# Weights folded at the last tile of statistics, a bias table from one selection matrix, and a reordered set-up of attention, in a two-layer block on one core

## The chip, the core and the metric

The kernel runs on one NeuronCore of a Trainium2 chip. The core has five engines with instruction streams of their own: TensorE (PE) multiplies matrices into PSUM, VectorE (DVE), ScalarE (ACT) and GpSimd (POOL) work elementwise, and SyncE (SP) issues most transfers; ACT can issue transfers too. Sixteen DMA engines carry the transfers. Engines wait for each other on semaphores only. The metric is the device time of one execution in microseconds (us). The kernel before takes 4699.47 us, the median of three runs (4699.33 to 4706.42).

## What is computed

The input x is 16 images of 56 x 56 pixels and 192 channels in float32. Two layers follow, each behind a group norm (32 groups over an image) and each added to its input:

```
x = x + L0(_gn(x))
x = x + L1(_gn(x))

L0(x): windows of 7 x 7 pixels; w = _ln(w, ln1_w, ln1_b)
       h_t = (w_t @ Bm) + h_(t-1) @ A          # over the 49 pixels of a window
       w = h @ Cm;  y = _ln(w, ln2_w, ln2_b)
       return w + gelu(y @ W1 + b1) @ W2 + b2
L1(x): roll by (-3, -3), windows of 7 x 7
       q, k, v = split(xw @ qkv_w.T + qkv_b)   # 12 heads of 16
       attn = q @ k.T / 4 + rpb_table[rel_idx] + shift_mask
       out = softmax(attn) @ v @ proj_w.T + proj_b;  roll back
```

`rpb_table` has 169 rows (13 x 13 relative positions) of 12 heads. `rel_idx` picks a row for each pair of the 49 pixels of a window, so the bias table of a head is 49 x 49.

## The kernel before

The program has three blocks, one after the other. At the end of a block every engine waits for all the others.

**Statistics of layer 0 and its weights.** x is read as 8 tiles of 128 windows by 49 pixels by 192 channels, 4.82 MB each. SP issues a load per tile into a ring of three buffers `xs` (line 147); the load of tile k waits until DVE has finished tile k - 2 (`s_bn`). DVE runs 32 BN_STATS on a tile, one per group (L204). The eleven loads of weights are issued by ACT on its own queue (L155, L157). Ahead of tile NT // 2, which is tile 4, DVE waits for all of them (`s_w`) and scales Bm and W1 by the weights of the layer norms (L198, L199). ACT then writes the upper parts of the weights (L162, L163) and POOL the lower parts (L175, L177); PE computes biases (L247, L251). After the last tile DVE, PE and POOL turn the statistics into tables (L208 to L235; POOL's power is L180).

**Layer 0.** 98 steps of 512 tokens. The last thing that a step does is the sum `x1` on DVE (L491). SP then stores it with 14 transfers (L379), seven for each half q of the partitions, into `x1_cells` in DRAM, while POOL adds it and its square to `acc_x` and `acc_x2` (L463 to L468). SP waits for the landing of all stores before the block ends (L383).

**Layer 1.** Its set-up stands in the code engine by engine. SP loads `hot0`, `hot1` (a one-hot matrix of 169 x 49 x 49, split at 128 rows), `groups`, `tab0`, `tab1` (the 169 rows of the table) and `mask`, all on semaphore `s_l` (L811), then the weights on `s_w3` (L816). It waits for `s_par`, and loads the tokens of units 0 and 1 and their parameters (L825, L826). DVE reduces the accumulators (L1024), PE averages over windows (L1130), DVE and POOL make mean and rstd (L1030 to L1036, L868), PE waits for all six of `s_l` and spreads them to channels (L1137), DVE copies (L1042, L1043), and PE projects the shifts through the weights (L1149) once `s_w3` is full. DVE makes `params` (L1050, L1052) and signals `s_par`. PE then gathers the bias table: for each of the 49 keys m two matmuls, `hot0` against `tab0` and `hot1` against `tab1`, with 12 columns (L1155, L1156). DVE meanwhile zeroes buffers (L1054 to L1059), copies the gathered table to both halves of the partitions (L1065) and adds the four masks (L1070), which sets `s_tabs`. PE waits for `s_tabs` before its first transposes (L1177). From there 256 units of four window pairs follow, of which nothing is changed.

## Time and profile before

| | us or share |
|---|---|
| median of three runs | 4699.47 |
| the profiled execution's own time | 4700.3 |
| its span | 4698.5 |
| statistics and weights, up to the first work of layer 0 | 0 to 151 |
| layer 0 | 151 to 2440.9 |
| set-up of layer 1 | 2440.9 to 2502 |
| units of layer 1 | 2502 to 4698.5 |
| busy shares: PE, DVE, ACT, POOL | 95%, 78%, 53%, 55% |
| mean granted clock of TensorE | 0.988 |

The busy shares are means over blocks that differ. PE's 95% is made in the 98 steps and the 256 units. In the slices of the page PE shows a 0 at the start and a 6 in the middle, which are the two places where it has next to nothing to do: the statistics and the set-up of layer 1. Times below are us from the start of the span. The execution takes 1.8 us more than its span.

### The profile page before, as it was taken

What the parts mean: (1) busy time and instruction counts of PE and PEld (TensorE: products, weight loads), DVE (VectorE), ACT (ScalarE), POOL (GpSimd) and SP (SyncE); (2) the same over time, 40 slices, a digit from 0 to 9 for tenths busy, and PEclk for the clock granted to TensorE, in tenths of its full rate; (3) what the DMA queues carried; (4) which work ended last, traced back from release to release, by engine and by line L of the source; (5) the groups of instructions that cost most, each with busy time, mean ns of one, the idle gap of its engine ahead of it and who ended that gap; (6) DMA issues with size and microseconds to landing.
All of it is one profiled execution on the core that took longest, in us unless ns stands there. A gap on an engine that the chain in (4) does not pass through costs nothing. (4 is left out here: it accounts for less than half of the span.)

```text
span 4698.5 us, 139967 instructions
## 1 busy us (share of the span) xinstructions
PE 4477.9 (95%) x51720; PEld 3760.2 (80%) x51720; DVE 3655.4 (78%) x7082; ACT 2497.3 (53%) x4850; POOL 2583.0 (55%) x2098
## 2 busy tenths in 40 slices
PE   0599999999999999999969999999999999999999
PEld 0488888888888888888857888888888888888887
DVE  6798888888888888888845777777777777777776
ACT  0244444444444444444424666666666666666666
POOL 1154455455445545545544666666666666666666
PEclk9999999999999999999988999999999999999999
DMA  8011111111111111111111222222222222222222
GB/s 346 22 39 38 38 38 40 39 39 41 38 38 39 39 39 39 41 38 38 40 45 48 73 72 70 72 72 70 71 71 70 71 72 72 72 70 72 72 70 62
DMA packets 389801, 286.01 MB, mean 61 GB/s; under 512 B 147163, under 2 KB 388043, under 8 KB 388555
## 3 DMA queue, kind: packets, MB, share of 16 engines
q1 hardware_dynamic: 387012, 283.15, 20.8%
q10 hardware_dynamic: 2736, 2.14, 0.1%
q8 instruction: 35, 0.57, 0.1%
q14 instruction: 18, 0.15, 0.0%
HBM read 120.34 MB, written 87.31 MB: 44 GB/s over the span
## 5 line engine op out<-in xcount | busy, mean ns | idle before, releaser
L894 POOL TENSOR_TENSOR L<-L,mx 128x588 f32<-128x588 f32 x512 | 601.3, 1175 | 747.7 <-DVE mx L1108 741.4
L1104 DVE SCALAR_TENSOR_TENSOR L<-ps_s,bias 128x588 f32<-128x588 f32 x512 | 394.7, 771 | 457.7 <-PE ps_s L1168 453.8
L603 PE MATMUL ps_o<-w,g_hi 128*128 128x384 f32 x2352 | 710.2, 365 | 5.9 <-DVE g_lo L543 4.1
L415 ACT ACTIVATE gF<-ps_g,b1f 128x512 f32<-128x512 f32 x588 | 405.9, 690 | 393.0 <-PE ps_g L634 390.5
L888 POOL TENSOR_TENSOR E<-E,ri 128x588 f32<-128x588 f32 x512 | 600.5, 1173 | 3.1 <-DVE ri L1114 3.1
L603 PE MATMUL ps_o<-w,g_lo 128*128 128x192 f32 x2352 | 534.4, 254 | 0.0
L975 ACT ACTIVATE PT<-ps_t 98x588 f32<-98x588 f32 x512 | 343.3, 671 | 325.9 <-PE ps_t L1243 322.9
L442 POOL TENSOR_TENSOR res<-xt,b2b 128x768 f32<-128x768 f32 x98 | 181.1, 1848 | 591.2 <-DVE x L491 591.2
L1168 PE MATMUL ps_s<-Kp,Q 32*64 32x98 f32 x12288 | 494.0, 259 | 3.6 <-DMA Kp<-K 2.7
L401 ACT ACTIVATE h_hi<-ps_h,hbias 128x512 fp32r<-128x512 f32 x196 | 123.3, 680 | 702.8 <-PE ps_h L618 702.8
L603 PEld LDWEIGHTS ps_o<-w,g_hi 128*128 128x128 f32 x2352 | 429.3, 189 | 26.5 <-issue 24.5
L603 PEld LDWEIGHTS ps_o<-w,g_lo 128*128 128x128 f32 x2352 | 443.8, 191 | 0.0
L1168 PEld LDWEIGHTS ps_s<-Kp,Q 32*64 32x64 f32 x12288 | 297.5, 130 | 158.2 <-issue 100.1
L1108 DVE TENSOR_REDUCE mx<-L 128x12 f32<-128x588 f32 x512 | 392.3, 766 | 17.5
L998 ACT ACTIVATE oT<-ps_v,vb 128x98 f32<-128x98 f32 (+1 forms) x1024 | 290.3, 335 | 216.4 <-PE ps_v L1275 216.4
L1217 PE MATMUL ps_w<-wp,oT 128*98 128x192 f32 x2048 | 396.3, 337 | 0.9 <-ACT oT L998 0.9
L1112 DVE TENSOR_REDUCE sm<-E 128x12 f32<-128x588 f32 x512 | 386.7, 755 | 1.5 <-ACT E L981 1.5
L1275 PEld LDWEIGHTS ps_v<-PT,Vx 98*32 98x32 f32 x12288 | 310.6, 150 | 93.6 <-issue 49.1
L1275 PE MATMUL ps_v<-PT,Vx 98*32 98x49 f32 x12288 | 374.7, 235 | 2.4 <-ACT PT L975 2.2
L452 POOL TENSOR_TENSOR g_lo<-gF,g_hi 128x512 fp32r<-128x512 f32 x196 | 251.1, 1303 | 198.6 <-ACT g_hi L420 198.6
L420 ACT ACTIVATE g_hi<-gF 128x512 fp32r<-128x512 f32 x588 | 355.4, 621 | 0.0
L981 ACT ACTIVATE E<-L 128x588 f32<-128x588 f32 x512 | 351.2, 686 | 3.6 <-POOL L L894 0.4
(210 smaller groups left out, 11761.5 us busy)
## 6 DMA issues: line engine op xcount, KB each, us to landing
xs<-in_x SPq DMA_DIRECT2D x8, 4704.0 KB, 22.5
xt<-in_x SPq DMA_DIRECT2D x98, 384.0 KB, 3.4
x_cells<-x SPq DMA_DIRECT2D x784, 48.0 KB
xb<-x_cells SPq DMA_DIRECT2D x128, 294.0 KB
Vx<-V SPq DMA_DIRECT2D x512, 73.5 KB
out<-yo SPq DMA_DIRECT2D x128, 294.0 KB
Kp<-K SPq DMA_DIRECT2D x256, 98.0 KB, 2.0
Kp<-K SPq DMA_DIRECT2D x256, 49.0 KB, 1.9
```

Of the source, the lines that this page charges most:

```text
L415: act.activation(gF[f % 4][:, :], ps_g[:, f % 2, :], ACT.Gelu, bias=b1f[:, f:f + 1]).then_inc(s_gelu, 1)
L420: act.activation(g_hi[:, g, :], gF[g % 4][:, :], ACT.Copy).then_inc(s_gh, 1)
L603: last = pe.matmul(dst, g[:, f, P * k:P * (k + 1)], w, start=(f == 0 and i == 0), stop=(f == FT - 1 and i == 1))
L888: pool.tensor_tensor(e, e, ri[p][:, :].unsqueeze(2).to_broadcast([P, HEADS, T]), ALU.mult)\
L894: pool.tensor_tensor(l, l, mx[p][:, :].unsqueeze(2).to_broadcast([P, HEADS, T]), ALU.subtract).then_inc(s_sub, 1)
L981: act.activation(E[pp][:, :, :], L[pp][:, :, :], ACT.Exp).then_inc(s_ex, 1)
L1104: dve.scalar_tensor_tensor(out=L[p][:, :, :].rearrange("p (a h) m -> p a (h m)", a=2), in0=ps_s[:, :, 0:SB], scalar=HD ** -0.5, in1=tab, o ...
L1108: dve.tensor_reduce(mx[p][:, :], L[p][:, :, :], AX.X, ALU.max).then_inc(s_mx, 1)
L1112: dve.tensor_reduce(sm[pp][:, :], E[pp][:, :, :], AX.X, ALU.add).then_inc(s_sm, 1)
L1168: last = pe.matmul(s_pair(j)[SLOT * w:SLOT * (w + 1)], Q[c][rows, chunk, 2 * p + w, :], Kp[c][rows, chunk, :, 2 * p + w, :], start=True, s ...
L1217: last = pe.matmul(ps_w(OUT1 if half else OUT0)[0:T2, C * a:C * (a + 1)], oT[d][p][:, k, :], wp[:, k, :], start=(k == 0), stop=(k == 1))
L1275: last = pe.matmul(ps_v[row:row + 2 * HD, col:col + T], Vx[lc][0:T2, 2 * lp + w, g:2 * HD * JP:JP], PT[lp % 2][0:T2, j, T * w:T * (w + 1)] ...
```

## The change

There are four edits.

1. DVE's wait for the weights and the folding stand ahead of the last tile of statistics (tile 7), no longer ahead of tile 4.
2. The seven stores of half q = 1 of the very last step are issued by ACT, which first waits for `s_x1`; SP issues the seven of q = 0. The code of a store becomes a function, which is otherwise the same.
3. The bias table is selected in another way. The table is loaded reversed. `tab` has 85 partitions by 49 keys by 12 heads: partition p holds for each key the row of the table that lies p rows behind the key's own first row. Four transfers write it. A matrix `query_row` of 85 x 128 has one 1 per query (for both halves of the partitions). Two matmuls of 504 and 84 columns then give the whole table, and two copies instead of four take it out. `hot0`, `hot1`, `tab0` and `tab1` are gone.
4. The set-up is in another order. PE gathers first, ahead of the averaging, and so waits for all seven loads of `s_l` before anything else. DVE zeroes its buffers in its waits, and its `base` copies stand ahead of the table of shifts. SP issues the tokens of unit 0 before its wait for `s_par`.

```diff
-                        if k == NT // 2:
+                        if k == NT - 1:
 
                             dve.wait_ge(s_w, 16 * WEIGHT_LOADS)
...
-                        for q in range(2):
+                        for q in range(1 if isinstance(n, int) and n == STEPS else 2):
+                            store(sp, d, u, q)
...
                 slots(act, slot)
+                act.wait_ge(s_x1, STEPS)
+                store(act, (STEPS - 1) % CHUNKS, (STEPS - 1) // CHUNKS, 1)
...
-            hot0, hot1 = sb("hot0", [P, T, T]), sb("hot1", [RPB - P, T, T])
-            tab0, tab1 = sb("tab0", [P, HEADS]), sb("tab1", [RPB - P, HEADS])
+            SPAN = 2 * WS - 1
+            REACH = (WS - 1) * (SPAN + 1) + 1
+            query_row, tab = sb("query_row", [REACH, P]), sb("tab", [REACH, T, HEADS])
...
+                for high in ((SHIFT, WS), (0, SHIFT)):
+                    for wide in ((SHIFT, WS), (0, SHIFT)):
+                        ny, nx = high[1] - high[0], wide[1] - wide[0]
+                        first = SPAN * ((high[0] - SHIFT) % WS) + (wide[0] - SHIFT) % WS
+                        rows = bass.AP(rpb.tensor, rpb.offset + HEADS * first,
+                                       [[HEADS, REACH], [HEADS * SPAN, ny], [1, nx * HEADS]])
+                        sp.dma_start(tab[:, :, :].rearrange("p (i j) h -> p i (j h)", i=WS)
+                                     [:, high[0]:high[1], HEADS * wide[0]:HEADS * wide[1]], rows).then_inc(s_l, 16)
...
-                sp.wait_ge(s_par, 1)
...
                     sp.dma_start(xb[c][0:T2, :, :], src).then_inc(s_xb[c], 16)
+                    if isinstance(u, int) and u == 0:
+                        sp.wait_ge(s_par, 1)
...
+                dve.memset(Kp[1][:, :, :, :, :], 0.0)
+                dve.memset(Vx[0][:, :, :], 0.0)
+                dve.wait_ge(s_b2, 1)
+                for b in range(2):
+                    m0, m1 = MB * b, min(MB * (b + 1), T)
+                    last = dve.tensor_copy(base[:, :, m0:m1],
+                                           ps_b[:, b, 0:(m1 - m0) * HEADS].rearrange("p (m h) -> p h m", h=HEADS))
+                link(last)
                 dve.wait_ge(s_p2, 1)
...
+                pe.wait_ge(s_l, 16 * 7)
+                for b in range(2):
+                    m0, m1 = MB * b, min(MB * (b + 1), T)
+                    last = pe.matmul(ps_b[:, b, 0:(m1 - m0) * HEADS], query_row[:, :],
+                                     tab[:, m0:m1, :].rearrange("r m h -> r (m h)"), start=True, stop=True)
+                last.then_inc(s_b2, 1)
                 pe.wait_ge(s_v2, 1)
...
-                for m in range(T):
-                    dst = ps_b[0:T, m // MB, (m % MB) * HEADS:(m % MB + 1) * HEADS]
-                    pe.matmul(dst, hot0[:, m, :], tab0[:, :], start=True, stop=False)
-                    last = pe.matmul(dst, hot1[:, m, :], tab1[:, :], start=False, stop=True)
-                last.then_inc(s_b2, 1)
```

DVE in the first block, before. `xs` are the tiles of x, `fold_B` and `fold_1` the scaled weights:

```order
L204 BN_STATS st<-xs2 128x6 x32
L204 BN_STATS st<-xs0 128x6 x32
L198 TENSOR_SCALAR fold_B<-raw_B,l1 128x192
L199 TENSOR_SCALAR fold_1<-raw_1,l2 128x768
L198 TENSOR_SCALAR fold_B<-raw_B,l1 128x192
L199 TENSOR_SCALAR fold_1<-raw_1,l2 128x768
L204 BN_STATS st<-xs1 128x6 x32
L204 BN_STATS st<-xs2 128x6 x32
L204 BN_STATS st<-xs0 128x6 x32
L204 BN_STATS st<-xs1 128x6 x32
L208 TENSOR_TENSOR pm<-st 128x256
```

The same stretch of DVE now:

```order
L204 BN_STATS st<-xs2 128x6 x32
L204 BN_STATS st<-xs0 128x6 x32
L204 BN_STATS st<-xs1 128x6 x32
L204 BN_STATS st<-xs2 128x6 x32
L204 BN_STATS st<-xs0 128x6 x32
L198 TENSOR_SCALAR fold_B<-raw_B,l1 128x192
L199 TENSOR_SCALAR fold_1<-raw_1,l2 128x768
L198 TENSOR_SCALAR fold_B<-raw_B,l1 128x192
L199 TENSOR_SCALAR fold_1<-raw_1,l2 128x768
L204 BN_STATS st<-xs1 128x6 x32
L208 TENSOR_TENSOR pm<-st 128x256
```

The four instructions that need the weights moved behind three more tiles of statistics.

PE in the set-up of layer 1, before, from its first instruction. `ps_w` and `ps_s` are PSUM; of L1155 and L1156 there are 49 pairs:

```order
L1130 MATMUL ps_w<-img_mean,pm 32x2 x16
L1137 MATMUL ps_w<-tab,groups 128x32
L1137 MATMUL ps_w<-tab,groups 64x32
L1149 MATMUL ps_w<-shift,raw_qkv 128x16 x6
L1149 MATMUL ps_w<-shift,raw_qkv 32x16 x12
L1155 MATMUL ps_s<-tab,hot 49x12
L1156 MATMUL ps_s<-tab,hot 49x12
```

PE there now:

```order
L1139 MATMUL ps_s<-tab,query_row 128x504
L1139 MATMUL ps_s<-tab,query_row 128x84
L1145 MATMUL ps_w<-img_mean,pm 32x2 x16
L1151 MATMUL ps_w<-tab,groups 128x32
L1151 MATMUL ps_w<-tab,groups 64x32
L1163 MATMUL ps_w<-shift,raw_qkv 128x16 x6
L1163 MATMUL ps_w<-shift,raw_qkv 32x16 x12
L1186 MATMUL ps_w<-ident,xb 128x98 x4
```

Two gathering matmuls stand first, and the transposes of unit 0 follow right behind the projection of the shifts.

SP's loads on `s_l`, before and then now:

```order
L811 DMA hot<-in_onehot 128x2401
L811 DMA hot<-in_onehot 41x2401
L811 DMA groups<-in_group_of 32x192
L811 DMA tab<-in_rpb 128x12
L811 DMA tab<-in_rpb 41x12
L811 DMA mask<-in_shift_mask 128x196
```

```order
L820 DMA tab<-in_rpb 85x4x48
L820 DMA tab<-in_rpb 85x4x36
L820 DMA tab<-in_rpb 85x3x48
L820 DMA tab<-in_rpb 85x3x36
L823 DMA query_row<-in_query_of 85x128
L823 DMA groups<-in_group_of 32x192
L823 DMA mask<-in_shift_mask 128x196
```

The one-hot rows are gone; four transfers of short runs (48 or 36 values) stand in their place.

## Rows read from the trace of the kernel before

**Rows 1.** Timeline of the first block: start, us, engine, line, operation [idle before <-releaser]

```profile
14.72 46.90 DVE L204 BATCH_NORM_STATS2 st<-xs 128x6 f32<-128x294 f32 x128 [14.72 <-DMA xs<-in_x]
...
88.51 0.32 DVE L198 TENSOR_SCALAR fold_B<-raw_B,l 128x192 f32<-128x192 f32 x1 [26.89 <-DMA raw<-in_W]
...
90.16 46.90 DVE L204 BATCH_NORM_STATS2 st<-xs 128x6 f32<-128x294 f32 x128
...
101.27 2.61 POOL L177 TENSOR_TENSOR w<-raw,w 128x1152 fp32r<-128x1152 f32 x1
...
143.42 1.02 POOL L180 TENSOR_TENSOR gtab<-gvar,neg_half 128x4 f32<-128x4 f32 x1 [39.53 <-DVE gvar L227]
```

**Rows 2.** DMA queues from 10 to 60 us: packets, MB, share of 16 engines

```profile
q1 hardware_dynamic: 638, 21.04, 97.8%
q10 hardware_dynamic: 639, 0.36, 2.3%
```

**Rows 3.** Stretches: length, five engines' busy time, PEclk, DMA share, GB/s

```profile
70.00:80.00 10.00, 0.00 (x0) 0.00 (x0) 0.00 (x0) 0.00 (x0) 0.00 (x0) 1.00 1.00 431
80.00:85.00 5.00, 0.00 (x0) 0.00 (x0) 0.00 (x0) 1.28 (x1) 0.00 (x0) 1.00 0.79 269
```

**Rows 4.** Timeline at the end of layer 0, SP's queue and POOL

```profile
2430.43 8.88 SPq L379 DMA_DIRECT2D x_cells<-x  x14
...
2433.62 1.80 POOL L468 TENSOR_TENSOR acc_x<-acc_x,x1sq 128x768 f32<-128x768 f32 x1
...
2440.92 0.72 SPq L811 DMA_DIRECT2D hot<-in_onehot  x2
```

**Rows 5.** Timeline of the set-up of layer 1

```profile
2442.96 10.54 SPq L811 DMA_DIRECT2D mask<-in_shift_mask  x1
...
2444.43 1.87 PE L1130 MATMUL ps_w<-img_mean,pm 128*32 128x2 f32 x32 [15.25 <-DVE pm L1024]
...
2447.24 2.90 POOL L868 TENSOR_TENSOR tab<-var,neg_half 32x16 f32<-32x16 f32 x1 [11.81 <-DVE var L1034]
...
2462.97 0.97 PE L1137 MATMUL ps_w<-tab,groups 32*128 32x32 f32 x4 [16.68 <-DMA mask<-in_shift_mask]
...
2464.95 5.99 PE L1149 MATMUL ps_w<-shift,raw_qkv 128*128 128x16 f32 x36 [1.01 <-DMA pbb<-in_proj_b]
...
2470.87 0.34 PE L1155 MATMUL ps_s<-tab,hot 128*49 128x12 f32 x2
...
2471.41 0.25 DVE L1052 COPY params<-ps_w 128x16 f32<-128x16 f32 x2
...
2472.08 0.55 SPq L826 DMA_DIRECT2D par<-params  x1
...
2473.74 1.36 DVE L1056 MEMSET Kp<- 128x1568 f32 x1 [0.28 <-issue]
...
2475.76 1.34 DVE L1059 MEMSET Vx<- 128x1536 f32 x1 [0.37 <-issue]
...
2497.24 1.67 DVE L1065 COPY base<-ps_s 49x504 f32<-49x504 f32 x4 [18.53 <-PE ps_s L1156]
...
2498.94 2.81 DVE L1070 TENSOR_TENSOR bias<-base,mask 128x588 f32<-128x588 f32 x4
...
2501.97 1.54 PE L1177 MATMUL ps_w<-ident,xb 98*128 98x98 f32 x8 [4.76 <-issue]
```

**Rows 6.** Stretches while the loads on `s_l` run; columns as in rows 3

```profile
2444.00:2445.00 1.00, 0.57 (x11) 0.58 (x12) 0.37 (x1) 0.00 (x0) 0.00 (x0) 0.50 1.06 451
...
2447.00:2449.00 2.00, 0.00 (x0) 0.00 (x0) 0.16 (x1) 0.00 (x0) 1.76 (x1) 0.50 0.07 29
```

**Rows 7.** SP's DMA queue, 2622.7 to 2623.2 (packets of 384 B) and 2438 to 2439 (mostly 768 B)

```profile
q1 hardware_dynamic: 116, 0.04, 35.3%
...
q1 hardware_dynamic: 112, 0.07, 29.5%
```

**Rows 8.** The costliest groups, page part 5: line, engine, operation, count | busy, mean ns

```profile
L1217 PE MATMUL ps_w<-wp,oT 128*98 128x192 f32 x2048 | 396.3, 337 | 0.9 <-ACT oT L998 0.9
```

More of the change, by code:

```diff
@@ L340, in there, with store @@
                 return not isinstance(n, int) or 0 <= n < STEPS
+            def store(engine, d, u, q):
+                i = u // WS
+                a, b = (WS + SHIFT - 1 - i) // WS, (WS + SHIFT - 1 - u % WS) // WS
+                imgs = slice(2 * TPC * d + q, 2 * TPC * (d + 1), 2)
+                base = q * WINS
+                rows, cols = bass.ds(1 - a, CELLS), bass.ds(1 - b, CELLS)
+                row, col = bass.ds(CELLS + 1 - a, 1), bass.ds(CELLS + 1 - b, 1)
+                parts = [(x1[d][base:base + WINS, k, :],
+                          x1_cells[rows, imgs.start + 2 * k, cols, bass.ds(u, 1), :]
+                          .rearrange("r w t c -> r w (t c)")) for k in range(TPC)]
+                parts += [(x1[d][base:base + CELLS, :, :],
+                           x1_cells[row, imgs, cols, bass.ds(u, 1), :]
+                           .rearrange("r k w t c -> (r w) k (t c)")),
+                          (x1[d][base:base + WINS:CELLS, :, :],
+                           x1_cells[rows, imgs, col, bass.ds(u, 1), :]
+                           .rearrange("r k w t c -> (r w) k (t c)")),
+                          (x1[d][base:base + 1, :, :],
+                           x1_cells[row, imgs, col, bass.ds(u, 1), :]
+                           .rearrange("r k w t c -> (r w) k (t c)"))]
+                for src, dst in parts:
+                    engine.dma_start(dst, src).then_inc(s_st[d], 16)
             block = ctx.enter_context(nc.Block())
@@ L808, in _ @@
             def _(sp):
-                for dst, src in ((hot0[:, :, :], onehot[0:P]), (hot1[:, :, :], onehot[P:RPB]),
-                                 (groups[:, :], group_of), (tab0[:, :], rpb[0:P]), (tab1[:, :], rpb[P:RPB]), (mask[:, :, :], shift_mask)):
+                for high in ((SHIFT, WS), (0, SHIFT)):
[6 more added lines that the diff above has]
+                                     [:, high[0]:high[1], HEADS * wide[0]:HEADS * wide[1]], rows).then_inc(s_l, 16)
+                for dst, src in ((query_row[:, :], query_of), (groups[:, :], group_of), (mask[:, :, :], shift_mask)):
                     sp.dma_start(dst, src).then_inc(s_l, 16)
@@ L1026, in _ @@
                 link(last)
+                dve.memset(Q[1][:, :, :, :], 0.0)
+                dve.memset(wp[CB:P, 1, :], 0.0)
+                link(dve.memset(params[:, :, :], 0.0))
                 dve.wait_ge(s_m2, 1)
```

56 lines of the change are left out of this document (11 added, 45 removed).

## Prediction

> **What bounds the kernel now.** I read the slices of the page first. PE is at nine tenths or more nearly everywhere, and none of its work there is edited, so the steps and units of both layers should keep their 4.49 ms. What can move is what lies between: the first 151 us and the middle. I read these in the timeline, then the DMA queues beside them.
>
> In the first block DVE sets the pace. It has 46.90 us of BN_STATS for four tiles, 11.73 us a tile, then sits idle for 26.89 us until the weights land at 88.51, folds for 1.65 us, and takes another 46.90 us [rows 1]. The weights are late because they share the engines with x: from 10 to 60 us x moved 638 packets and the weights 639 [rows 2], one for one, at 37.6 KB against well under 1 KB. The wait is thus for the stream of x to dry up, and it dries up because DVE waits: the DMA share is 1.00 up to 80 us and 0.79 in the next five [rows 3].
>
> At the end of layer 0 SP issues 14 stores in 8.88 us, one each 0.63 us; the next block begins 1.61 us behind the last of them, at 2440.92 [rows 4]. POOL was done at 2435.42.
>
> The set-up of layer 1 takes 61.05 us from there to the first transposes at 2501.97 [rows 5]. Its chain is: the loads on `s_l`, which PE awaits until 2462.97; a further DMA wait; the projection of 5.99 us; 98 gathering matmuls from 2470.87 to 2497.2; the copies of 1.67 us; the masks of 2.81 us [rows 5]. The load that holds everything is the one-hot part with 41 partitions: at first all 16 engines are busy (share 1.06), then for some ten us the share is 0.07 at 29 GB/s, one engine of 16 [rows 6].
>
> **Edit 1, the folding.** DVE reaches tile 7 at 14.72 + 7 x 11.73 = 96.8. Is x there in time? Tile 7 may be requested when tile 4 is done, at 73.4, while the stream is still full. It is 4.82 MB, at 431 GB/s [rows 3] 11.2 us, and lands some 11 us behind the end of the stream near 81, about 92 to 93: in time. The weights now wait behind that tile as well: 88.51 + 11.2, less about 0.3 for the eight weight packets per engine that slip through beside it, is 99.4. So DVE idles from 96.8 to 99.4, folds until 101.1, and ends tile 7 at 112.8, where it ended at 137.06 before. **Gain 24.3 us.** ACT's and POOL's splitting now lies behind the fold: POOL ended 103.88, 13.7 us behind the fold's end at 90.16 [rows 1], so it would end at 114.8. The power on POOL is due 6.3 us behind the last tile (137.1 to 143.42) [rows 1], at 119.1; the cover is 4.3 us, and if it went, every us beyond would cost one. PE's biases take 8 us and are hidden likewise. Bounds: 22, if the weights land at 101.7, and 26.9, if DVE's idle time vanishes altogether.
>
> **Edit 2, the stores.** SP's seven take 4.43 us, until 2434.9. ACT's seven run beside them; no row shows ACT issuing such a store, so between SP's 0.63 us each and, if the two queues hindered each other fully, the old 8.88 us for both. A packet of 768 B keeps an engine busy 0.295 x 16 x 1 us / 112 = 42 ns [rows 7]; 648 packets over the 8 rows that a store spans are 3.4 us, less than the issue time, so I take 0.63 to 0.7. The block then starts near 2435.2 + 1.6 = 2436.8; POOL's end at 2435.42 is the floor. **Gain 4.1 us**, bounds 0 and 4.9. Behind ACT's new wait nothing is queued, since these were its last instructions of the block.
>
> **Edit 3, the new loads.** This is the dear unknown. The four transfers of `tab` have 85 x 14 = 1190 runs of 192 or 144 B. Two things are needed: the cost of a packet and the number of engines. Packets of 384 B take 0.353 x 16 x 0.5 us / 116 = 24 ns of an engine [rows 7], and shorter ones should not be dearer by much. From above, engine 0 had still 59 small packets behind the one-hot rows (41 x 9.6 KB at 29 GB/s, to about 2459.4) and all had landed by 2462.97, so no more than 61 ns each [rows 5, 6]. I take 30, nearer to the measured packet. On the engines: 128 partitions used all sixteen, 41 used one [rows 6]. I read that as a cut into equal shares of partitions; 85 is 5 x 17, so five engines with 238 packets each, 7.1 us. With 1.5 us until data flows, 27 packets more for `query_row`, `groups` and `mask` (0.9 us) and about 0.5 to 1 us of landing, `s_l` is full **10.0 us** after the block's start (call it L). At 24 ns it is 8.9, at 61 ns 18.6.
>
> The Trainium skill, "DMA: Bandwidth & Descriptors", section on why a DMA increments its semaphore by 16, says that the engine count is the largest number up to 16 that divides the slowest dimension of both sides. By that rule, the trace agrees: 41 gives one. Without any such rule, spread evenly over sixteen, L would be 5.4 and the sum 4.6 us better. Under "Specifications" the same page says that a transfer under 512 B costs a read-modify-write. The row of 384 B does not show it, at 24 ns against 42 for 768 B; were each short packet doubled to 48 ns, L would be 14.8 and the sum 4.8 us worse.
>
> **Edit 4, the new chain**, from the block's start, with handovers of about 0.1 us. All terms but three are from [rows 5]:
> - L, 10.0. PE now waits for it before everything. DVE's reduction (3.41 us) and three memsets are over by 5.4, so the averaging, which ran at 3.5 before, is what is queued behind that wait. This costs the chain 6.5 us plus the gather.
> - The gather: 588 columns. An f32 matmul of 192 columns takes 337 ns at the full clock [rows 8], and the clock here is 0.50 [rows 6], thus 3.5 ns a column: 2.1.
> - Averaging 1.87, then DVE's four small steps until POOL could start, 0.94.
> - POOL's power 2.90 is now beside DVE's two memsets, 1.36 + 1.34, and two copies, half of 1.67, with gaps 4.1. The longer, 4.1, counts. One small step, 0.23.
> - L1137's matmuls 1.07; DVE's copies and the handover, at most the 1.01 that stood there.
> - The projection 5.99 + 0.1. Its weights on `s_w3` are issued once the queue drains, near L - 2, and need some 6 to 7 us, by 15; the projection is due at 21. Hidden, with 6 us of cover.
> - `params` 0.72; the masks 2.81 + 0.07; handover 0.22. The load of `par` (0.55 and at most the 1.6 us that a store takes to land [rows 4]) is beside the masks, and the tokens of unit 0 are already there.
>
> The sum is 31.1 us, against 61.05: **gain 29.9 us**. What leaves is the gather of 26.3 us and most of a 16.68 us wait; what comes is the wait for `tab`. With L from 8.9 to 18.6 the gain is 31.0 to 21.3. PE's clock is at 0.50 in this stretch before, and I expect it there again, with no change for unit 0.
>
> **Sum.** 24.3 + 4.1 + 29.9 = 58.3 us. The profiled execution took 4700.3, so 4642.0; it lies 0.8 us above the median of the runs, so **4641 us**.
>
> **Rivals.**
> - **`tab` comes late.** If the 1190 packets went over one engine as those of 41 partitions did, they take 28.6 us at 24 ns and L is about 32: 22 us worse, 4663. Five engines at 100 ns a packet give nearly the same. For it: no row shows such short runs from DRAM spread over a count like 85. Against: 48 B rows were taken at under 61 ns.
> - **The weights stay starved.** ACT's queue refills only as it drains, and DVE waits for weights to 110 instead of 99.4. Then 4652. For it: the last weights were requested only at 81, when x dried up. Against: from there to the landing took 7.5 us, and nothing slows that now.
> - **The long loops shift.** Their buffers have other addresses and another start. They are 95% of the time; 0.2% of them is 9 us, either way: 4632 or 4650. Against: no instruction in them differs.
> - **Slower.** A packet of `tab` costs a full round of its engine, with nothing overlapped. The only packets seen alone on an engine, the 9.6 KB ones, took 326 ns. At that price 265 packets take 86 us, L is 89 and the kernel 4720. It decides from 68 us for L, about 250 ns a packet. Against: the 384 B rows at 24 ns.
> - **Nothing is won at the start.** DVE's idle time moves whole behind tile 6. That needs weights at 123, with nothing on the queues by then: left at 0.01 or less.
>
> **How the numbers follow.** Forecast 0.76, `tab` late 0.11, weights starved 0.05, loops 0.04 (half each way), slower 0.03, nothing at the start 0.01. The forecast's own bounds add to 22 + 0 + 21.3 and 26.9 + 4.9 + 31.0, but not all ends meet at once; 4634 to 4656 holds them. The range reaches from 4632 to 4659, which leaves out most of the late `tab` and the slower case. A difference under 0.2%, 9.4 us, could not be told from no change. Faster by more: 0.96; within: 0.01; slower: 0.03.
>
> **What would show it.** DVE idle for some 3 us ahead of L198, near 97, and the first step of layer 0 near 127. The set-up's first transfer near 2412 on the new clock (24 + 4 us earlier than 2440.92). The two gathering matmuls about 10 us behind it, released by DMA. The first transposes 31 us behind it, released by DVE's masks. I would be wrong if the DMA view showed `tab` at one engine's share for 20 us and more, if POOL's L180 waited for L177, or if the 256 units took another time than 2196.5 us.

## The result: 4643.9 us, and the profile after

The changed kernel takes 4643.86 us, median of four runs (4638.18 to 4645.91), against 4702.94 for the kernel before on the same chip (4699.33 to 4706.47). The ratio is 0.9872, 95% interval 0.9855 to 0.989: faster by 59 us. The forecast was 4641 us, range 4632 to 4659. The profiled execution of the changed kernel took 4643.41 us, with a span of 4641.6.

The span of before is 4698.5. The 56.9 us between the two spans lie here:

| stretch | before | after | gain | forecast |
|---|---|---|---|---|
| start to the first load of layer 0 | 151.33 | 129.93 | 21.4 | 24.3 |
| from there to the end of the last x1 | 2279.03 | 2279.76 | -0.7 | 0 |
| x1 to the first transfer of the next block | 10.56 | 7.16 | 3.4 | 4.1 |
| block's start to the first transposes | 61.05 | 26.23 | 34.8 | 29.9 |
| the 256 units and the end | 2196.5 | 2198.5 | -2.0 | 0 |

First the timeline of the first block in the changed kernel (start, us, engine, line, operation; in brackets the idle time before it and what ended it). It answers to [rows 1].

```profile
100.47 0.32 DVE L198 TENSOR_SCALAR fold_B<-raw_B,l 128x192 f32<-128x192 f32 x1 [3.54 <-DMA raw<-in_W]
...
113.23 2.61 POOL L177 TENSOR_TENSOR w<-raw,w 128x1152 fp32r<-128x1152 f32 x1
113.94 2.36 DVE L208 TENSOR_TENSOR pm<-st 128x256 f32<-128x256 f32 x1
116.33 0.61 DVE L209 TENSOR_TENSOR sq<-st 128x256 f32<-128x256 f32 x1
...
122.02 1.02 POOL L180 TENSOR_TENSOR gtab<-gvar,neg_half 128x4 f32<-128x4 f32 x1 [6.18 <-DVE gvar L227]
```

DVE's wait of 26.89 us has become one of 3.54. The line to look at is DVE's L208, though: L208 and L209 have the same shape and the same kind, and one took 2.36 us, the other 0.61. L208 was due while POOL had its subtract of 2.61 us in hand, and ended 0.46 us after it.

Now SP's and ACT's queues at the end of layer 0 and the start of the next block; this answers to [rows 4].

```profile
2409.72 5.51 ACTq L363 DMA_DIRECT2D x_cells<-x  x7
2409.76 4.54 SPq L363 DMA_DIRECT2D x_cells<-x  x7
...
2416.85 2.19 SPq L820 DMA_DIRECT2D tab<-in_rpb  x4
...
2420.06 0.41 SPq L823 DMA_DIRECT2D mask<-in_shift_mask  x1
```

A store costs ACT 5.51 / 7 = 0.79 us to issue, where SP needs 0.65, and the block begins 1.6 us behind ACT's last. The mask's issue, which took 10.54 us before [rows 5], takes 0.41: the queue no longer blocks.

The set-up of layer 1, in order of time; this answers to [rows 5].

```profile
2422.16 2.40 PE L1139 MATMUL ps_s<-tab,query_row 85*128 85x504 f32 x4 [13.65 <-DMA mask<-in_shift_mask]
2424.49 1.87 PE L1145 MATMUL ps_w<-img_mean,pm 128*32 128x2 f32 x32
...
2427.30 2.90 POOL L880 TENSOR_TENSOR tab<-var,neg_half 32x16 f32<-32x16 f32 x1 [12.55 <-DVE var L1049]
...
2431.53 0.97 PE L1151 MATMUL ps_w<-tab,groups 32*128 32x32 f32 x4 [5.17 <-DVE tab L1059]
...
2433.46 5.97 PE L1163 MATMUL ps_w<-shift,raw_qkv 128*128 128x16 f32 x36 [0.96 <-DVE shift L1065]
...
2440.07 2.80 DVE L1079 TENSOR_TENSOR bias<-base,mask 128x588 f32<-128x588 f32 x4
...
2443.08 1.54 PE L1186 MATMUL ps_w<-ident,xb 98*128 98x98 f32 x8 [3.65 <-issue]
```

The gather starts 5.31 us behind the block's first transfer; the forecast had put the full semaphore at 10.0. The gather takes 2.33 us where 2.1 were forecast, and behind it every link stands within 0.2 us of its forecast.

A window while `tab` lands (length, five engines' busy time, PEclk, DMA share, GB/s), to set beside [rows 6]:

```profile
2418.00:2419.00 1.00, 0.00 (x0) 0.00 (x0) 1.00 (x2) 0.00 (x0) 0.00 (x0) 0.50 0.37 69
```

A share of 0.37 is near five or six engines of 16. Beside them, the row of SP's DMA queue from 2418 to 2420 (packets, MB, share):

```profile
q1 hardware_dynamic: 797, 0.13, 36.4%
```

That is 0.364 x 16 x 2 us / 797 = 14.6 ns of an engine for a packet of about 160 B. The forecast had taken 30. By the clock it is less: with five engines at work, 2 us x 5 / 797 = 12.5 ns from one packet to the next. The share, 0.36 where five engines of 16 are 0.31, counts packets that overlap on one engine more than once.

### The profile page after: what moved, and what is told of

Read it like the earlier page. It is cut to its first block and busy times, and to the rows that moved or that the text cites. A ratio compares the mean times of both kernels' runs of the same rounds, so it can differ in the third digit from the quotient of the medians.

```text
span 4641.6 us, 139580 instructions
## 1 busy us (share of the span) xinstructions
PE 4452.8 (96%) x51528; PEld 3736.3 (80%) x51528; DVE 3655.4 (79%) x7079; ACT 2496.8 (54%) x4850; POOL 2583.2 (56%) x2098
## 3 DMA queue, kind: packets, MB, share of 16 engines
q1 hardware_dynamic: 387564, 281.52, 20.9%
```

## The experiments

Each is an edit of one of the two kernels. Times of single executions scatter by some 4 us either way (the four runs of the changed kernel span 7.7), so the verdicts below rest on stretches of the profiled execution, not on totals. Where three or five rounds are named, the total is a median of four executions. "The gap" is from the end of the last x1 to the next block's first transfer; "the turn" is the first transposes, counted from that transfer.

### One part at a time

**The folding alone**, in the kernel before:

```diff
-                        if k == NT // 2:
+                        if k == NT - 1:
```

> The kernel before with edit 1 alone (folding ahead of tile 7). My theory: the first block's gain is the 26.89 us of idle time less what comes back, and the same 21.4 us as with all edits: the weights land at about 100.5, layer 0's first load is issued at 129.9 instead of 151.33, and everything behind it is shifted only (block start to first transposes 61.05 us as before). L208 on DVE takes 2.36 us instead of 0.61, because POOL's L177 now runs beside it. Rival: L208's length comes from something that the other edits changed; then it is 0.61 here and the load is issued at 128.2.

Measured: 4686.03 us beside 4708.38. The weights landed at 100.08, the first load of layer 0 went out at 129.53, and L208 took 2.35 us beside POOL's L177. So the long L208 belongs to this edit alone. The gap (10.55) and the turn (60.8) were those of before.

**The stores alone**, in the kernel before:

```diff
+                        for q in range(1 if isinstance(n, int) and n == STEPS else 2):
+                            store(sp, d, u, q)
...
+                act.wait_ge(s_x1, STEPS)
+                store(act, (STEPS - 1) % CHUNKS, (STEPS - 1) // CHUNKS, 1)
```

> The kernel before with edit 2 alone (seven last stores issued by ACT). My theory: the last x1 to the next block's first transfer takes 7.16 us instead of 10.56, set by ACT's seven issues at 0.79 us each; the first block stays at 151.3 and the set-up at 61.05 us. Rival: the gain is made by the lighter loads of the next block, and the gap stays near 10.5 us here.

Measured: the gap is 7.15 us (2431.37 to 2438.52), as in the changed kernel, against 10.56. The total, 4706.47, hardly shows it.

**The table alone**, in the kernel before; PE's gather stays last in its order, behind the projection:

```diff
-                for m in range(T):
...
+                for b in range(2):
+                    m0, m1 = MB * b, min(MB * (b + 1), T)
+                    last = pe.matmul(ps_b[:, b, 0:(m1 - m0) * HEADS], query_row[:, :],
+                                     tab[:, m0:m1, :].rearrange("r m h -> r (m h)"), start=True, stop=True)
```

> The kernel before with edit 3 alone: the new selection matrix and table, gathered where the old one was gathered, and every memset and wait in the old order. My theory: nearly all of the set-up's gain is this edit. Averaging at 3.5 us from the block's start, the power until 9.2, L1137's matmuls until 10.7, the projection until 17.3, params 18.0, then the gather of 2.4 and DVE's 6.7 us of memsets behind params until 24.7, two copies until 25.6, masks until 28.5: first transposes at 28.7 us, against 61.05 before and 26.23 with all edits. The order alone is then worth 2.5 us. Rival: the order is worth much more, because the loads on s_w3 or the tokens come late; then the transposes stand at 35 us or later.

Measured: 4670.69 us; the turn at 27.97 us (2441.39 to 2469.36). The whole reordering of the changed kernel is worth the remaining 1.7 us; the table does the rest, 33.1. The average of 1.87 us ran at 3.50 here, before `tab` was needed.

### What sets the start of the gather

**83 partitions and 2** in place of 85, everything else the same:

```diff
-                for high in ((SHIFT, WS), (0, SHIFT)):
-                    for wide in ((SHIFT, WS), (0, SHIFT)):
+                for p0, p1 in ((0, 83), (83, REACH)):
+                    for high in ((SHIFT, WS), (0, SHIFT)):
+                        for wide in ((SHIFT, WS), (0, SHIFT)):
...
-                pe.wait_ge(s_l, 16 * 7)
+                pe.wait_ge(s_l, 16 * 11)
```

> The changed kernel, with each of the four loads of tab cut into 83 and 2 partitions (same bytes, same 1190 runs of 192 and 144 B). Theory of the prediction: the partitions are cut into equal shares, so 83, which has no factor, goes to one engine. At the 12.5 ns per packet and engine of the changed kernel (797 packets in 2 us on five engines), 1162 packets take 14.5 us, and the gather starts at about 17 us from the block's start instead of 5.3; the DMA share is near 0.07 in between. Rival: engines are used alike whatever the count; the gather starts at 6 to 7 us, later by the four further issues alone.

SP's own queue in the timeline:

```profile
2413.59 13.90 SPq L821 DMA_DIRECT2D tab<-in_rpb  x8
```

Two windows, the first while it is stuck:

```profile
2422.00:2428.00 6.00, 0.00 (x0) 0.00 (x0) 0.00 (x0) 0.00 (x0) 0.00 (x0) 0.50 0.08 15
2428.00:2430.00 2.00, 0.00 (x0) 0.00 (x0) 0.00 (x0) 0.00 (x0) 0.00 (x0) 0.50 0.46 103
```

And the row of SP's DMA queue from 2416 to 2428:

```profile
q1 hardware_dynamic: 1089, 0.18, 8.2%
```

The gather came 16.75 us behind the block's start instead of 5.31, and the total was 4653.01. A share of 0.08 is little more than one engine of 16. So the count of partitions decides over how many engines a load is cut: 83 gives one, 85 gave five. The forecast's five engines were right. Here the issue itself is held, 13.90 us for eight transfers. A packet costs 0.082 x 16 x 12 us / 1089 = 14.5 ns by the share, as in the changed kernel, and 12 us / 1089 = 11.0 ns by the clock if one engine takes them all.

**96 partitions**, a multiple of 16, with the tables padded:

```diff
-            query_row, tab = sb("query_row", [REACH, P]), sb("tab", [REACH, T, HEADS])
+            ROWS = 96
+            query_row, tab = sb("query_row", [ROWS, P]), sb("tab", [ROWS, T, HEADS])
```

> The changed kernel, with tab and the selection matrix on 96 partitions instead of 85 (the eleven further rows of the matrix are zero, the table is padded with zeros). Theory A: the 5.3 us until the gather are SP's issues (3.6 us to the end of the seventh) and the landing of the last (1.6 us); sixteen engines instead of five change nothing, 5.0 to 5.5 us. Theory B: they are the 238 packets on each of five engines; then 84 packets on each of sixteen save 1.9 us, 3.4 us.

```profile
2418.60 2.40 PE L1139 MATMUL ps_s<-tab,query_row 96*128 96x504 f32 x4 [13.34 <-DMA mask<-in_shift_mask]
```

A window of it, 1.4 to 2.4 us behind the block's start:

```profile
2415.00:2416.00 1.00, 0.00 (x0) 0.00 (x0) 1.00 (x2) 0.00 (x0) 0.00 (x0) 0.50 0.71 128
```

The gather starts 5.01 us behind the block's start (2413.59), against 5.31. The share goes up to 0.71, so more than five engines work, and yet that brings 0.3 us only. What counts is SP: in the changed kernel it hands over its seventh load at 2420.06 to 2420.47, 3.6 us behind the start, and PE runs 1.7 us later. Here the seventh is handed over 3.3 us behind the start (the issues are a little shorter), and PE again runs 1.7 us later, so even the 0.3 us comes from the issues. The releaser named in both is the mask, the last load issued. The one execution took 4640.5 us.

**The average ahead of the gather** in PE's order:

```diff
-                pe.wait_ge(s_l, 16 * 7)
-                for b in range(2):
...
                 pe.wait_ge(s_v2, 1)
                 for a in range(2):
...
                 last.then_inc(s_m2, 1)
+                pe.wait_ge(s_l, 16 * 7)
+                for b in range(2):
...
                 pe.wait_ge(s_v2, 8)
```

> The changed kernel, with PE's wait for the loads and the gather moved behind the averaging matmuls (one piece of edit 4 undone). My theory: in the changed kernel the wait of 5.3 us for the loads and the gather of 2.3 us stand on the chain that sets the end of the set-up, while DVE had been ready at 3.5 us. Here the averaging runs at 3.5 and the gather under POOL's power, and the first transposes come 4.1 us earlier: 22.1 us from the block's start instead of 26.2. Rival: the copies of base on DVE then become what the chain waits for, and the place stays at 25 to 26 us.

```profile
2420.37 1.87 PE L1139 MATMUL ps_w<-img_mean,pm 128*32 128x2 f32 x32 [11.84 <-DVE pm L1036]
2422.63 2.40 PE L1146 MATMUL ps_s<-tab,query_row 85*128 85x504 f32 x4 [0.39 <-DMA mask<-in_shift_mask]
```

The turn is at 22.05 us, 4.2 earlier, as expected: the averaging no longer stands behind `s_l`, and the gather lies beside POOL's power. Yet the total was 4643.18, the changed kernel's own. The 256 units behind it took 2202.5 us instead of 2198.5. That question is taken up below.

### POOL and DVE

**POOL's subtract behind its power:**

```diff
-                    pool.tensor_tensor(w2[:, :, 1, :], raw_2[:, :, :], w2[:, :, 0, :], ALU.subtract)
...
                     pool.tensor_tensor(gtab[:, 0, :, :], gvar[:, :, :],
                                        neg_half[:, :].rearrange("p (a b) -> p a b", a=2), ALU.pow).then_inc(s_pow, 1)
+                    pool.tensor_tensor(w2[:, :, 1, :], raw_2[:, :, :], w2[:, :, 0, :], ALU.subtract)
```

> The changed kernel, with POOL's last subtraction for W2 (L177, 2.61 us) behind its power (L180) instead of ahead of it. In the changed kernel L177 ran from 113.23 to 115.84 and DVE's L208 from 113.94 to 116.30, 2.36 us where it had taken 0.61. Theory: L208 stands still until L177 ends, since each reads two operands from SBUF. Then L208 takes 0.61 us here and layer 0's first load is issued 1.7 us earlier, at 128.2. Rival: L208 is long because it starts right behind BN_STATS that is not yet written out, or because of L175; then it is 2.4 us again.

Measured: the first load of layer 0 at 130.13, where 128.2 was expected, and 4641.96 us in all. The add on `pm` took 0.61 us, as the theory wanted, but:

```profile
120.88 2.61 POOL L180 TENSOR_TENSOR w<-raw,w 128x1152 fp32r<-128x1152 f32 x1
121.01 2.50 DVE L228 TENSOR_TENSOR gtab<-gmean,gtab 128x4 f32<-128x4 f32 x1 [1.20 <-POOL gtab L178]
```

A multiply of 128x4 elements, 0.16 us otherwise, stands for 2.50. Its size does not help it; it has two inputs in SBUF, and POOL had begun 0.13 us earlier.

**POOL's subtract behind DVE's table**, timed in five rounds:

```diff
                                        neg_half[:, :].rearrange("p (a b) -> p a b", a=2), ALU.pow).then_inc(s_pow, 1)
+                    pool.wait_ge(s_fold, 13)
+                    pool.tensor_tensor(w2[:, :, 1, :], raw_2[:, :, :], w2[:, :, 0, :], ALU.subtract)
```

> The changed kernel with POOL's last subtract of the weights (128x1152, 2.61 us) put behind the widened table of the vector engine (gwide, which ends at 123.77 in the changed kernel). Just behind the power, the same subtract had held a 128x4 multiply of the vector engine for 2.50 us; ahead of it, the 128x256 add for 2.36. Theory, the two engines stand in each other's way only while both run an instruction with two inputs from SBUF: here the subtract lies at 122.0 to 124.6 beside TensorE's 2.1 us of matmuls and at most the first 0.4 us of a copy out of PSUM, so the add and the multiply take 0.61 and 0.16, the first load of layer 0 comes at 128.2 (129.93 in the changed kernel), and the total is 1.75 less. Rival, any instruction of POOL with two inputs holds any of the vector engine's: the copy out of PSUM starts late or lasts longer by what is left of the subtract (up to 0.4), and the load comes at 128.6. Rival, the subtract holds the end of the block: load at 129.9 or later. In the total only five rounds could show 1.75 us, and the scatter of the granted clock in the first and last units (0 to 5 us each) is larger: 4641 to 4643 expected.

```profile
113.61 0.61 DVE L208 TENSOR_TENSOR pm<-st 128x256 f32<-128x256 f32 x1
...
121.06 0.16 DVE L229 TENSOR_TENSOR gtab<-gmean,gtab 128x4 f32<-128x4 f32 x1 [1.20 <-POOL gtab L178]
...
121.76 2.61 POOL L181 TENSOR_TENSOR w<-raw,w 128x1152 fp32r<-128x1152 f32 x1 [0.81 <-DVE gwide L230]
123.92 1.76 DVE L235 COPY R<-ps_g 128x1536 f32<-128x1536 f32 x1 [2.23 <-PE ps_g L265]
127.84 0.94 SPq L374 DMA_DIRECT2D xt<-in_x  x2
```

The add takes 0.61 and the multiply 0.16. The copy out of PSUM began 0.45 us before the subtract was over, and took its usual 1.76. The first load went out at 127.84, 2.09 us earlier than in the changed kernel: 1.75 from the add, the rest from a last tile that ended 0.3 earlier. So the add and the multiply, with both inputs in SBUF, are held by the subtract, and the copy out of PSUM is not.

"Two inputs from SBUF on both sides" is not the whole rule, though. The trace of the changed kernel has counterexamples both ways in the steps of layer 0; here lines of one step, first POOL's power beside a subtract of DVE that has both inputs in SBUF, then a TENSOR_SCALAR of DVE with one tensor input, before POOL's subtract and beside it:

```profile
1001.99 1.02 POOL L452 TENSOR_TENSOR rsa<-vea,neg_half 128x4 f32<-128x4 f32 x1
1002.56 0.69 DVE L536 TENSOR_TENSOR g_lo<-gF,g_hi 128x512 fp32r<-128x512 f32 x1 [0.65 <-ACT g_hi L423]
...
1004.33 0.37 DVE L541 TENSOR_SCALAR xn<-xn,mva,rsa 128x192 f32<-128x192 f32 x1
...
1004.90 1.43 DVE L541 TENSOR_SCALAR xn<-xn,mva,rsa 128x192 f32<-128x192 f32 x1
1004.93 1.30 POOL L457 TENSOR_TENSOR g_lo<-gF,g_hi 128x512 fp32r<-128x512 f32 x1 [1.91 <-ACT g_hi L423]
```

The power does not hold DVE's subtract, which takes 0.69 us in all its 196 executions, beside the power or not. The TENSOR_SCALAR (one tensor and two columns of scalars, all in SBUF) takes 0.37 us alone and 1.43 beside POOL's subtract, so it is held too. Over the 98 steps, the 103 of its 392 executions that have no POOL operation beside them take 0.369 to 0.379 us, and the 102 that begin inside one take 1.339 to 1.849. No run here has a POOL operation with one tensor input. Which forms collide has to be read from a trace of these forms.

The total, 4643.25 us (4641.51 to 4644.85), ratio 0.9876 with an interval of 0.9859 to 0.9892, cannot be told from the changed kernel's.

**The weights on SP's queue**, between the loads of tiles 5 and 6, folded ahead of tile 6:

```diff
+                        if k == NT - 3:
+                            for dst, src in ((raw_B[:, :, :], Bm.rearrange("(k p) n -> p k n", p=P)),
...
+                                             (b2b[:, :], b2.partition_broadcast(P))):
+                                sp.dma_start(dst, src).then_inc(s_w, 16)
...
-                    for raw, src in ((raw_B, Bm), (raw_A, A), (raw_C, Cm), (raw_1, W1)):
-                        act.dma_start(raw[:, :, :], src.rearrange("(k p) n -> p k n", p=P)).then_inc(s_w, 16)
...
-                        if k == NT - 1:
+                        if k == NT - 2:
```

> The changed kernel, with the six large weight loads issued by SP behind the load of tile 5 instead of by ACT beside x, and the folding ahead of tile 6. Theory: the weights are late only because each of their packets waits for one packet of x of 37.6 KB. In one queue they take about 5 us, land near 75, and DVE never idles more than a us; POOL's part ends near 101, so that L208 has nothing beside it (0.61 us). DVE then ends tile 7 near 110.5 instead of 113.9, and layer 0's first load is issued near 124.7 instead of 129.93. Rival: x and weights together are more than the DMA engines can carry in time, and DVE waits for x at tiles 6 and 7 for as long as it waited for weights before; then the load is issued at 128 or later.

```profile
89.25 23.14 DVE L208 BATCH_NORM_STATS2 st<-xs 128x6 f32<-128x294 f32 x63 [2.62 <-DMA xs<-in_x]
```

DVE no longer waits for the weights, but now 2.62 us for tile 6, which came behind them. The first load of layer 0 is at 127.03: better than 129.93, by 1.1 us up to the end of tile 7 (0.9 of it less waiting) and 1.75 of collision (POOL was done at 100.4), and not the 124.7 hoped for. The bytes in front of the last tile are the same in any order, and the DMA engines had no room to take them faster: from 50 to 90 us their share is 0.94 or more but for 0.79 from 68 to 70.

### The granted clock behind the turn

The one execution of that kernel took 4632.76 us, 10.7 less than the changed kernel's profiled one, though the turn came only 6.2 earlier. With the averaging first it was the reverse. Part of it lies in layer 0, whose steps no edit here touches: from its first load to the last x1 it took 2276.3 us in that kernel and 2279.8 in the changed one, and 2275.8 to 2280.2 over all the kernels of this document. So of the 6.2 us, 2.9 are the edit's and 3.5 are layer 0's, less 0.2 that the set-up took longer. For the rest I read the units in windows. In the first 56 us and in the last 40, PE's granted clock stands at times at 0.50, that is 1.2 of 2.4 GHz; in between it is 1.00, but for 1.7 us' worth in one kernel (the last below). Summing PE's busy time times (1 - clock) over windows of 4 us there (20 us in between) gives an estimate of the time lost:

| kernel | the units | lost at first | lost in between and last | rest |
|---|---|---|---|---|
| before | 2196.5 | 4.1 | 3.1 | 2189.3 |
| changed | 2198.5 | 5.8 | 0.0 | 2192.8 |
| average first | 2202.5 | 11.1 | 1.4 | 2190.0 |
| 96 partitions | 2199.2 | 6.1 | 0.0 | 2193.2 |
| POOL late | 2200.8 | 4.1 | 5.6 | 2191.1 |
| weights on SP | 2194.2 | 4.0 | 0.0 | 2190.2 |
| weights and average (below) | 2205.4 | 9.7 | 4.5 | 2191.3 |
| 83 partitions and 2 | 2199.9 | 8.7 | 1.5 | 2189.7 |
| POOL behind the table | 2200.8 | 7.5 | 1.5 | 2191.8 |

The units differ by 11.3 us among these kernels; the rest, less these losses, by 3.9. Windows from the turn on, and of the last 40 us (columns as above), first of the changed kernel:

```profile
2443.08:2451.08 8.00, 6.46 (x27) 6.09 (x28) 1.25 (x2) 3.02 (x6) 0.00 (x0) 0.55 0.10 26
2451.08:2467.08 16.00, 11.23 (x184) 8.98 (x182) 9.95 (x16) 9.18 (x15) 10.02 (x9) 1.00 0.23 65
2467.08:2475.08 8.00, 7.01 (x109) 5.75 (x104) 2.73 (x5) 3.78 (x9) 3.04 (x5) 0.57 0.04 15
2475.08:2499.08 24.00, 24.00 (x422) 19.50 (x420) 17.40 (x30) 16.41 (x34) 14.76 (x14) 1.00 0.27 72
4601.00:4641.60 40.60, 33.05 (x636) 26.82 (x631) 23.57 (x41) 21.94 (x49) 23.29 (x20) 1.00 0.17 48
```

then of the kernel with the average first:

```profile
2438.91:2446.91 8.00, 6.46 (x23) 6.11 (x24) 1.24 (x2) 2.91 (x5) 0.00 (x0) 0.50 0.11 29
2446.91:2462.91 16.00, 12.80 (x163) 10.35 (x161) 9.32 (x15) 9.01 (x14) 7.94 (x8) 0.89 0.20 54
2462.91:2478.91 16.00, 14.24 (x179) 11.30 (x180) 7.30 (x13) 6.34 (x14) 8.63 (x8) 0.57 0.19 53
```

The same instructions, but the second stretch at half clock lasts 16 us and not 8. There the 4.2 us went, in this execution. Whether the averaging's place has a part in it is open: both kernels with the average first lost most at first (11.1 and 9.7 us), but the two last rows of the table, with the set-up in the changed kernel's order, lost 8.7 and 7.5. The four runs of the changed kernel differ in the same way without any edit: the mean granted clock was 0.994 in the run of 4638.18 us, 0.992 in that of 4645.91, and 0.993 in the other two.

**Spare work on PE**, in the changed kernel, timed in three rounds:

```diff
                 slots(pe, slot)
+                for _ in range(20):
+                    pe.matmul(ps_h[:, 0, 0:P], ident[:, :], ident[:, :], start=True, stop=True)
...
+                def spin(n):
+                    for _ in range(n):
+                        pe.matmul(ps_v[:, 0:P], ident[:, :], ident[:, :], start=True, stop=True)
+
+                spin(12)
                 pe.wait_ge(s_l, 16 * 7)
...
+                spin(12)
                 pe.wait_ge(s_v2, 8)
...
                 last.then_inc(s_q2, 1)
+                spin(8)
```

> The changed kernel with spare TensorE work, whose result nobody reads, in the gaps of its set-up of attention: the identity times itself (128 columns), 20 times behind layer 0's last matmul (8.6 us idle to the block's start), 12 at the block's start, 12 ahead of the wait for the image table, 8 behind the projection. In question is why 4 us won ahead of the units did not show in the total. In windows of 4 us from the first transposes on, the granted clock is below 1.00 in four windows of the changed kernel (by busy time, 5.8 us lost), in seven of the one with the average ahead of the gather (11.1), in three of the one with the weights on SP's queue (4.0). Theory A, the clock there follows what TensorE did before: with dense work ahead, it is 1.00 from within the set-up on; averaging 1.87 to 0.94 us, gather 2.4 to 1.2, projection 5.97 to 3.0, so first transposes 20.6 us from the block's start (26.2 in the changed kernel), and the units lose none of the 5.8: total 11.3 less, 4632 beside 4643. Rival B, the clock falls at the change of layer and comes back by itself whatever TensorE does (in the kernel before it stood at 0.50 through 16 us of busy matmuls): durations stay, the spare matmuls at 0.3 to 0.4 us each just fit the gaps, total 4643 to 4647. Rival C, the spare work holds up the queue: first transposes later than 26.2.

PE in the set-up, in the timeline:

```profile
2413.35 4.54 PE L1140 MATMUL ps_v<-ident 128*128 128x128 f32 x24 [3.94 <-PEq L96]
2418.82 1.30 PE L1146 MATMUL ps_s<-tab,query_row 85*128 85x504 f32 x4 [0.93 <-DMA mask<-in_shift_mask]
2420.05 1.17 PE L1152 MATMUL ps_w<-img_mean,pm 128*32 128x2 f32 x32
...
2427.97 5.96 PE L1171 MATMUL ps_w<-shift,raw_qkv 128*128 128x16 f32 x36 [0.95 <-DVE shift L1067]
```

Two windows of it:

```profile
2417.00:2421.00 4.00, 3.07 (x43) 2.33 (x42) 1.28 (x3) 0.00 (x0) 0.00 (x0) 1.00 0.80 230
...
2428.00:2434.00 6.00, 6.00 (x37) 5.34 (x37) 1.38 (x2) 0.00 (x0) 3.64 (x7) 0.50 0.00 1
```

Half of theory A holds. The clock did rise in the set-up, to 1.00, and the gather fell from 2.40 to 1.30 us. But by the projection it was down to 0.50 again, and stayed there through 6.00 us in which the records show PE busy throughout, with matmuls of 16 columns. The turn came at 24.26 us instead of 26.23 (20.6 expected). At the start of the units the clock was 1.00 for the transposes and then fell as before; 4.6 us were lost there, 3.1 at the end. The total is 4639.83 us (4638.69 to 4644.62), ratio 0.9871, interval 0.9854 to 0.9887: no difference from the changed kernel that could be told.

**The weights on SP's queue and the average first**, three rounds; the edits are those shown.

> Two edits tried before, together: the weights behind the loads of x on SP's queue, folded at the last tile but one (first block 2.9 us shorter, no collision of POOL and DVE on pm), and the average ahead of the gather (first transposes 22.1 us from the block's start, 4.1 to 4.2 less). Expected: first load of layer 0 at 127.0, first transposes 22.1 from the start. If the units cost what they cost with the weights edit alone (2194.2): 4632.8 - 4.2 = 4628.6. If the first units again lie at the half clock for as long as with the average ahead alone (2202.5): 4636. By the first theory of the clock (what TensorE did before) nothing says which, so both stand; a measured time above 4638 would say that the edits take from each other.

Measured: 4637.41 us (4633.31 to 4642.64), ratio 0.986, interval 0.9844 to 0.9877. The first load is at 127.67, the turn at 22.07 us, 2434.36 on the clock, 8.7 ahead of the changed kernel. Both gains add up, 2.3 and 4.2 us; the other 2.3 lie in layer 0. In the profiled execution, of 4642.64 us, the two draws of the clock were poor ones, 14.2 us together:

```profile
2458.36:2474.36 16.00, 14.68 (x175) 11.77 (x177) 6.68 (x11) 5.91 (x13) 6.60 (x7) 0.57 0.17 45
...
4599.80:4639.80 40.00, 32.81 (x568) 26.37 (x567) 20.17 (x35) 19.06 (x42) 19.80 (x18) 0.87 0.15 42
```

By medians it is the fastest of those timed in rounds, and well below the kernel before. That it beats the changed kernel, by 6.4 us where the stretches say 6.5, is likely and not shown: the intervals overlap.

**The same with spare work**, three rounds, 20, 8, 8 and 8 matmuls:

> The same two edits with the spare TensorE work (20 behind layer 0, 8 at the block's start, 8 behind the gather, 8 behind the projection). Theory A (clock follows TensorE's work): first transposes at 22.1 - 0.9 (averaging) - 1.2 (gather) - 0.5 (image table) - 3.0 (projection) = 16.5 us from the start if the vector engine's own steps do not end last, units without the 4 to 11 us lost at the half clock, so 4628.6 - 5.6 - 4 = 4619, and down to 4615. Theory B (clock comes back by itself): as the kernel without the spare work, 4628 to 4638.

```profile
2410.16 3.75 PE L1144 MATMUL ps_v<-ident 128*128 128x128 f32 x16 [3.93 <-PEq L96]
...
2415.75 2.40 PE L1157 MATMUL ps_s<-tab,query_row 85*128 85x504 f32 x4
...
2421.57 0.98 PE L1164 MATMUL ps_w<-tab,groups 32*128 32x32 f32 x4
```

The gather shows the half clock's duration, 2.40, and so did the averaging, 1.87: the clock had not risen. The spare work ran at 0.46 us a matmul, longer than the gaps it was meant for, so L1164 came 11.46 us behind the start instead of 10.54, and the turn at 23.01 instead of 22.07. This is rival C of the first run with spare work. The total is 4640.76 us (4639.10 to 4641.70), above what either theory gave. Why the clock rose in the run with 12 spare matmuls at the start and not in this one, these runs do not tell.

## Why the prediction was right, and where its steps were off

The total was off by 2.9 us, and the sign and place of all three gains were right. That it came so near is in part luck. Two of the three gains lie outside the bounds that the working gave them, on opposite sides: 21.4 us at the start (22 to 26.9) and 34.8 in the set-up (21.3 to 31.0).

- **What bounds the kernel.** Right. The units and the steps of layer 0 took what they had taken, within 2.0 and 0.7 us, which is less than they differ by among the kernels above.
- **Edit 1, 24.3 forecast, 21.4 measured.** The weights landed at 100.47, not 99.4: ACT could issue the last of them at 93.17, 12.2 us later than before (80.97), where the working had 11.2 less 0.3. Its choice of tile was right: the load of tile 7 waits for the end of tile 4, since the semaphore counts finished tiles from 1, so that the load of tile k waits for tile k - 3 in the numbering from 0. The rest is a step that was missing: "the cover is 4.3 us" looked only at whether POOL would be late for its power. It was not (it waited 6.18 us). But POOL's work was moved to where DVE has adds with two inputs from SBUF, and L208 stood for 1.75 us more. The Trainium skill, "SBUF — State Buffer", section "Who interferes with whom", calls the ports that both engines share an exclusive lock, for which a DVE instruction with two inputs from SBUF contends with a POOL instruction that reads SBUF. The trace agrees for these two: 2.36 and 2.50 us beside a subtract of 2.61, and 0.61 and 0.16 without it. For POOL's power, which reads SBUF too, it does not: beside it DVE's subtract of two inputs from SBUF took 0.69 us, as without it.
- **Edit 2, 4.1 forecast, 3.4 measured.** The step was the price of a store on ACT, "0.63 to 0.7": it is 0.79, and seven of them set the block's start.
- **Edit 3, L of 10.0 forecast, 5.31 measured.** Five engines was right. The 5.4 that the working gave for packets spread over sixteen fits 5.31 by the number only: the share was 0.37 in the changed kernel and 0.71 with 96 partitions. "I take 30" was the mis-sized term: 14.6 ns by the share. The upper bound of 61 ns had pulled the choice above the row of 24 ns; the packets are of half that row's size and cost about half. With 238 packets at that price an engine is done within 3.5 us, and another limit takes over, SP's own issues, 3.6 us, and 1.7 to the gather. "This costs the chain 6.5 us plus the gather" thus became 1.8 plus the gather's 2.3, which is what the average ahead of it won back, 4.2. (The bounds of L, 8.9 and 18.6, take a landing of 1 us, the 10.0 one of about 0.55.)
- **Edit 4, 31.1 forecast, 26.23 measured**, 4.7 of it L. From the gather on it is 20.9 against 21.1: 2.33 for 2.1 in the gather, and less in the copies, the projection, `params` and the masks. The clock was at 0.50 as expected. The projection's weights stayed hidden.
- **"No change for unit 0."** Wrong by size. Neither the kernel's instructions nor their order changed there, but the clock's first stretch lost 5.8 us in place of 4.1, and the last 0.0 in place of 3.1; the rest of the units was 3.5 longer, partly by PE's idle time at first (7.3 against 5.3 us in 56). The working had named another time than 2196.5 as a sign of being wrong; as the units took 2194.2 to 2205.4 among kernels that leave them as they are, 2198.5 says nothing for or against the change.
- **The rivals.** `tab` over one engine is what 83 partitions give: 16.75 us, not 32, since a packet costs less than the 24 ns taken; that kernel took 4653, not 4663. The starved weights did not occur. The slower case would have needed 250 ns a packet.

## What to carry to other kernels

When work is moved to cover a wait, look not only at whether it is done in time but at what the engine beside it runs meanwhile: beside a subtract of POOL, DVE's operations with two inputs from SBUF stood still until it was over, and so did a TENSOR_SCALAR from SBUF. Even an operation of 128x4 elements then costs what is left of POOL's. Put such work of POOL beside DVE's BN_STATS (11.80 us for the tile beside POOL's subtracts, 82.00 for the seven before it), beside its copies out of PSUM, or beside its waits.

Choose the partitions of a load so that they fall on many engines (85 or 96, not 83), and once that is done count the issues: seven small loads cost SP 3.6 us whatever their packets cost.

A gain of 4 us ahead of a long stretch of matmuls is to be read from the stretch where it is made. The total of one execution moves by more than that with the granted clock behind every pause of TensorE.

## What the runs showed of the hardware that was not expected

- The clock behind a pause of TensorE differs from kernel to kernel though the units are the same: 4.0 to 11.1 us lost in the first 56 us of the units, 0.0 to 5.6 near the end. The Trainium skill, "TensorE: Matmul & The Clock Gate", Part 1, says that the number of matmuls at the half clock differs from run to run. The changed kernel's four runs agree, with a mean granted clock of 0.992 to 0.994; its trace shows beside it a second fall some 16 us behind the first rise (0.57 over 8 us, and over 16 with the average first).
- Packets of some 160 B cost 14.5 ns of an engine by the share, with five engines or one at work, where 384 B cost 24 and 768 B 42 [rows 7]. By the clock one followed another within 11.0 to 12.5 ns.
- A queue whose packets all lie on one engine holds its issuer: eight loads took SP 13.90 us to hand over, with the DMA share at 0.08, and in the kernel before the mask's load took 10.54 [rows 5], with the share at 0.07 [rows 6].
- DVE's TENSOR_SCALAR of 128x192 from SBUF takes 0.37 us, and 1.43 beside a subtract of POOL, though only one input is a tensor. Out of PSUM the same form takes 0.47 us, beside POOL's adds too.
- Matmuls of 16 columns, back to back for 6 us, left the clock at 0.50, and so did those of 12 columns in the kernel before, with PE recorded busy throughout both. A window of before, inside its 98 gathering matmuls:

```profile
2478.00:2494.00 16.00, 16.00 (x121) 14.24 (x121) 0.71 (x1) 0.00 (x0) 0.00 (x0) 0.50 0.00 1
```
